# Layer-1 expert tiles loaded in pairs into ten slots, and the attention softmax taken by head from PSUM

## The reference

```
# layer 0
x += ssm(layernorm(x))                       # gated linear recurrence over time
x += xattn(layernorm(x), ctx, mask0)         # 16 heads of 16, 64 keys
x += layernorm(x) @ (W + V_r C).T + b
# layer 1
x += lstm_positions(layernorm(x))            # LSTM of 20 units, 512 steps; weights over earlier positions
x += xattn(layernorm(x), ctx, mask1) with weights * fside after the softmax
x += moe(layernorm(x))                       # 8 experts, top 1; leaky relu, squared; hidden 128

# the softmax of both attentions
scores = q @ k.T / 4
scores = where(mask0, scores, finfo.min)     # layer 0
scores = scores + (1 - mask1) * -1e9         # layer 1
attn = softmax(scores)                       # layer 1: then attn * fside
```

## Time and profile before

| | us |
|---|---|
| median of 3 runs (3178.17 to 3192.34) | 3188.12 |
| the profiled execution, its own time | 3191.33 |
| its span, first to last instruction | 3189.5 |

### The profile page before, as it was taken

How to read it: one execution, slowest core, us unless ns; L and a number is a source line. 1 busy time by engine, 2 the same in 40 slices (tenths; PEclk the granted TensorE clock), 3 DMA queues, 4 the chain that set the end, 5 groups by cost and what they waited for, 6 DMA issues and landing times.

```text
span 3189.5 us, 39732 instructions
## 1 busy us (share of the span) xinstructions
PE 2584.9 (81%) x11385; PEld 1542.6 (48%) x11385; DVE 1893.2 (59%) x6517; ACT 853.2 (27%) x2341; POOL 1317.4 (41%) x1372
## 2 busy tenths in 40 slices
PE   5799896977778778778778787999998868887945
PEld 3466453543636354635354545544544535544533
DVE  4576787768685767586768686645655414242311
ACT  0233242332232233223232332212222212122211
POOL 0363342324443345334444453423432545555534
PEclk9999896978786887678878786999899889899965
DMA  4110101020101110201010101111111253433032
GB/s 160 54 62 13 49 12 38 1 71 14 48 24 39 33 53 25 58 20 58 20 57 20 57 14 47 34 41 34 33 40 36 71 119 90 127 96 100 27 92 81
DMA packets 195337, 164.88 MB, mean 52 GB/s; under 512 B 52913, under 2 KB 188171, under 8 KB 194896
## 3 DMA queue, kind: packets, MB, share of 16 engines
q1 hardware_dynamic: 182352, 137.55, 14.6%
q0 software_dynamic: 12800, 25.27, 2.8%
HBM read 118.81 MB, written 51.80 MB: 53 GB/s over the span
## 4 chain that ended last, share of the span: by engine, by line
PE 36%; issue 21%; DVE 19%; POOL 12%; DMA 6%; SPq 3%; ACT 2%; POOLq 0%; DVEq 0%; ACTq 0%
PE p L775 4%; PE p L869 4%; PE p L832 4%; PE p L808 4%; PE p L769 3%; DVE l_xnat L1185 3%; PE p L786 3%; DMA out<-xy,xid 3%; DMA xw<-in_w_proj 3%; PE p L822 2%; POOL l_scratch L1547 2%; PE pg L841 2%; DVE ln_stats L1160 2%; PE p L849 2%; POOL l_scratch L1542 2%
## 5 line engine op out<-in xcount | busy, mean ns | idle before, releaser
L1521 POOL TENSOR_TENSOR ln_rstd<-ln_ve,neghalf 128x4 f32<-128x4 f32 x96 | 98.2, 1023 | 714.6 <-DVE ln_ve L1169 713.2
L1535 POOL TENSOR_TENSOR l_kbd<-l_kg,headmask 128x512 f32<-128x512 f32 x256 | 266.8, 1052 | 305.5 <-PE p L808 210.7
L1465 DVE SCALAR_TENSOR_TENSOR uin<-gates 16x20 f32<-16x20 f32 x512 | 175.5, 343 | 283.4 <-ACT gates L987 281.5
L832 PEld LDWEIGHTS p<-l_vg,l_scratch 128*128 128x128 f32 x2048 | 282.2, 215 | 75.0 <-issue 36.6
L987 ACT ACTIVATE gates<-pg 16x80 f32<-16x80 f32 x512 | 114.9, 224 | 761.0 <-PE pg L841 759.4
L1542 POOL TENSOR_TENSOR l_scratch<-l_scratch,l_mx 128x512 f32<-128x512 f32 x256 | 265.3, 1042 | 117.5 <-DVE l_mx L1215 116.7
L832 PE MATMUL p<-l_vg,l_scratch 128*128 128x34 f32 x2048 | 292.7, 296 | 15.9 <-ACT l_scratch L1016 6.8
L769 PE MATMUL p<-ident,l_xnat 128*128 128x128 f32 x1024 | 202.0, 339 | 123.2 <-DVE l_xnat L1185 122.0
L841 PE MATMUL pg<-wcat,slots 128*16 128x80 f32 x1024 | 177.2, 260 | 150.9 <-DVE slots L1477 149.0
L808 PE MATMUL p<-l_kbd,l_qT 128*128 128x512 f32 x512 | 275.6, 628 | 10.9 <-DVE l_scratch L1211 9.7
L841 PEld LDWEIGHTS pg<-wcat,slots 128*16 128x16 f32 x1024 | 59.0, 97 | 387.9 <-DVE slots L1477 238.5
(11 more groups left out here) (209 smaller groups left out, 4723.6 us busy)
## 6 DMA issues: line engine op xcount, KB each, us to landing
xln<-xln_dram SPq DMA_DIRECT2D x40, 512.0 KB, 4.4
l_vg<-v_dram SPq DMA_DIRECT2D x32, 544.0 KB, 4.0
x_dram<-l_xres SPq DMA_DIRECT2D x32, 512.0 KB, 3.6
xw<-in_w_fc SPq DMA_DIRECT2D x84, 128.0 KB, 2.2
xw<-in_w_proj SPq DMA_DIRECT2D x84, 128.0 KB, 2.5
l_kg<-k_dram SPq DMA_DIRECT2D x32, 256.0 KB, 4.3
xln_dram<-l_xnat SPq DMA_DIRECT2D x16, 512.0 KB, 3.0
l_xres<-x_dram SPq DMA_DIRECT2D x16, 512.0 KB, 5.5
```

The lines of the kernel that those rows point to most:

```text
L832: i = pe.matmul(o_bank[l][:, q * VW:(q + 1) * VW], w.exT[:, j, p, :], w.vg[:, b, q * VW:(q + 1) * VW], start=True, stop=True)
L1465: dve.scalar_tensor_tensor(uin[:, :], gates[:, 0:20], 1.0, gates[:, 60:80], ALU.add, ALU.mult)
L1535: pool.tensor_tensor(w.kbd[b % 2][:, j, :, :], w.kg[:, j, b:b + 1, :].broadcast_to([P, NE, SK]), headmask[:, :].rearrange("p (a o) -> p a ...
```

## The change

**Expert tiles.** Ten slots instead of four, and four output buffers instead of two. The slots take no new SBUF: weights go into the tiles of layer-0 weights (`wA` to `wO[0]`) and `tiles[0].xres`, rows into `tiles[0].xnat`, `xT`, `qT` and `kbd`, all free once lane 0 has ended. Two tiles are one step of SyncE; a pair shares the semaphores `m_in` and `m_rows`, so the first gather waits for the loads of both tiles and the first transpose for both gathers. The load of tile q waits for the expert matmul and scatter of tile q-10.

**Softmax.** `neg` becomes bf16 and its sign and that of q are turned, so that PSUM holds the negated scores. The mask is added on TensorE: a matmul of a bf16 identity (`same`) with `neg` broadcast over the 8 heads opens the accumulation, the score matmul closes it. VectorE takes the minimum from PSUM. ScalarE computes exp(-s + minimum) from PSUM with the minimum as per-partition bias, one instruction per head, 8 per unit, planned as four steps of two. "mask" and "shift" are gone. The next score into a bank waits for the eighth exp (`exped`), not for the mask. The sums stay on VectorE.

**Planner.** Costs are changed (see the diff), the hop after a DMA from 3 to 7 us, TILE_EVERY from 3.5 to 2.8 us. The spread is no longer given: `planned` tries 72 to 144 in steps of 8 and keeps the shortest plan. Stage 6 joins the stages with filler matmuls. Some semaphores are merged, and `orow` needs "keys" 7 instead of "shift" 7.

The core of the diff:

```diff
-TILE_SLOTS = 4
+TILE_SLOTS, OUT_SLOTS = 10, 4
...
-            ("pe", "score", u, 0.85, [("qland", u % 2), ("keys", u), ("mask", u - 2)]),
-            ("dve", "mask", u, 0.6, [("score", u), ("neg", 0), ("pturn", u - 4)] + ([("rows", 3)] if u == 0 and ahead else [])),
-            ("dve", "max", u, 0.6, [("mask", u)]),
-            ("pool", "shift", u, 1.0, [("max", u)]),
-            ("act", "exp", u, 0.5, [("shift", u)])]
+            ("pe", "score", u, 1.1, [("qland", u % 2), ("keys", u), ("neg", 0), ("exp", 4 * (u - 2) + 3)]),
+            ("dve", "max", u, 0.65, [("score", u), ("exp", 4 * (u - 4) + 3)] + ([("rows", 3)] if u == 0 and ahead else []))]
+        steps += [("act", "exp", 4 * u + e, 0.45, [("max", u), ("pturn", u - 4)])
+                  for e in range(4)]
...
+    for p in range(count // 2):
+        steps += [
+            ("clock", "due", p, 2 * every, [("due", p - 1)]),
+            ("sp", "mload", p, 5.6, [("due", p - 1), ("mexpert", 2 * p + 1 - TILE_SLOTS), ("mscatter", 2 * p + 1 - TILE_SLOTS)]),
+            ("dma", "mids", p, 0.1, [("mload", p)])]
+        steps += [("pool", "mgather", k, 1.3, [("mids", p), ("madd", k - TILE_SLOTS)]) for k in (2 * p, 2 * p + 1)]
+        steps += [("dma", "mrows", p, 0.1, [("mgather", 2 * p + 1)])]
...
-HOPS = {"pe": 0.22, "act": 0.2, "dve": 0.18, "pool": 0.1, "sp": 0.2, "dma": 3.0, "clock": 0.0}
-
-PACE = {0: (0.0, 4.0, 0.4), 1: (96.0, 16.0, 0.6), 2: (128.0, 4.0, 0.3), 3: (140.0, 0.0, 0.4), 4: (112.0, -18.0, 0.35),
-        5: (0.0, 22.0, 0.4), 6: (0.0, 0.0, 0.4)}
+HOPS = {"pe": 0.22, "act": 0.2, "dve": 0.18, "pool": 0.1, "sp": 0.2, "dma": 7.0, "clock": 0.0}
+
+PACE = {0: (4.0, 0.4), 1: (16.0, 0.6), 2: (4.0, 0.3), 3: (0.0, 0.4), 4: (-18.0, 0.35), 5: (22.0, 0.4), 6: (0.0, 0.4)}
...
-TILE_EVERY = 3.5
+TILE_EVERY = 2.8
...
-IDLE, FILL, WARM = 0.3, 0.9, (0, 4, 5)
+IDLE, FILL, WARM = 0.3, 0.9, (0, 4, 5, 6)
...
+    spreads = range(72, 152, 8) if 1 <= stage <= NC_ else (0,)
+    return min((planned_at(stage, ahead, spread) for spread in spreads), key=lambda plan: plan[0])[1]
...
-                        pe.wait_ge(t.masked, N - 1)
+                        pe.wait_ge(t.exped, N - 1)
+                    if u == 0:
+                        pe.wait_ge(t.neg, m + 1)
+                    pe.matmul(banks[l][j], same[:, :], w.neg[:, b:b + 1, :].broadcast_to([P, NE, SK]), start=True, stop=False)
                     pe.wait_ge(t.kbd, N + 1)
                     pe.matmul(banks[l][j], w.qT[:, j, b * P:(b + 1) * P],
-                              w.kbd[b % 2][:, j, :, :].rearrange("p a k -> p (a k)"), start=True, stop=True
+                              w.kbd[b % 2][:, j, :, :].rearrange("p a k -> p (a k)"), start=False, stop=True
                               ).then_inc(t.scores, 1)
...
-                    act.activation(ex, ex, ACT.Exp).then_inc(t.exped, 1)
...
+                    for h in (2 * e, 2 * e + 1):
+                        i = act.activation(w.ex[b % 2][:, NE * j + h, :], banks[lane][j][:, h * SK:(h + 1) * SK], ACT.Exp, scale=-1.0,
+                                           bias=w.mx[:, u % 4, h:h + 1])
+                    if e == 3:
+                        i.then_inc(t.exped, 1)
```

More of the change, by code:

```diff
@@ L38 @@
 EPS = 1e-5
[L39 removed]
+FMAX = 3.3895313892515355e38
 VW = 2 * HD + 2
@@ L120, in __init__ @@
         self.q, self.q_ready, self.kbd = sem(f"{name}_q"), sem(f"{name}_q_ready"), sem(f"{name}_kbd")
-        self.scores, self.masked, self.top = sem(f"{name}_scores"), sem(f"{name}_masked"), sem(f"{name}_top")
-        self.shifted, self.exped, self.summed = sem(f"{name}_shifted"), sem(f"{name}_exped"), sem(f"{name}_summed")
+        self.scores, self.top = sem(f"{name}_scores"), sem(f"{name}_top")
+        self.exped, self.summed = sem(f"{name}_exped"), sem(f"{name}_summed")
         self.gated, self.turned, self.exT = sem(f"{name}_gated"), sem(f"{name}_turned"), sem(f"{name}_exT")
@@ L189, in attention_steps @@
             ("dve", "o", u, 0.2 if l else 0.45, [("pv", u)] + ([("sums", u)] if l else []))]
-    steps += [("pool", "orow", 0, 2.3, [("shift", 7)])]
-    steps += [("pe", "oturn", h, 0.45, [("o", 4 * h + 3), ("mask", 7)]) for h in range(2)]
+    steps += [("pool", "orow", 0, 2.3, [("keys", 7)])]
+    steps += [("pe", "oturn", h, 0.45, [("o", 4 * h + 3), ("exp", 31)]) for h in range(2)]
     steps += [("act", "oland", h, 0.5, [("oturn", 1)]) for h in range(2)]
@@ L368, in planned @@
         kept.append((who, *key))
-    return kept
+    return max(end.values()), kept
 PLANS = {(stage, ahead): planned(stage, ahead) for stage in range(NC_ + 3) for ahead in (False, True)
@@ L443, in decoder_program @@
         tri = sb("tri", [P, P])
+        same = sb("same", [P, P], BF16)
         headmask = sb("headmask", [P, NE])
@@ L516, in decoder_program @@
         steps_row = sb("steps_row", [1, 2, 64])
-        xw = [sb(f"xw{i}", [P, 2 * D]) for i in range(TILE_SLOTS)]
-        xg = [sb(f"xg{i}", [P, 2 * D]) for i in range(TILE_SLOTS)]
+        whole = lambda w: w[:, :, :].rearrange("p h n -> p (h n)")
+        xw = [whole(w) for w in (wA, wB, wC, wD, wOut, wF, wQ[0], wO[0])]
+        parts = lambda w: [w[:, i:i + 2 * D] for i in range(0, 4 * D, 2 * D)]
+        done = tiles[0]
+        xw += parts(whole(done.xres))
+        xg = parts(whole(done.xnat)) + parts(whole(done.xT)) + parts(whole(done.qT))
+        xg += [t for w in done.kbd for t in parts(w[:, :, :, :].rearrange("p h a k -> p (h a k)"))]
         xid = [sb(f"xid{i}", [P, 2], I32) for i in range(TILE_SLOTS)]
@@ L523, in decoder_program @@
         xq = [sb(f"xq{i}", [P, P]) for i in range(2)]
-        xy = [sb(f"xy{i}", [P, D]) for i in range(2)]
+        xy = [sb(f"xy{i}", [P, D]) for i in range(OUT_SLOTS)]
         ctxA = xln[:, :, :, :].rearrange("p i b d -> p (i b d)").rearrange("p (h b k) -> p h b k", h=NH, b=B)
@@ L726, in _ @@
                             sp_step(lane, layer, family, index, c, g, n, m)
-            for i in range(2):
-                sp.wait_ge(o_store[i], 16 * (EARLY * TILES[0] + TILES[1]) // 2)
+            for i in range(OUT_SLOTS):
+                sp.wait_ge(o_store[i], 16 * (EARLY * TILES[0] + TILES[1]) // OUT_SLOTS)
         @block.tensor
@@ L793, in attention_step @@
                     if i_ == 0:
-                        pe.wait_ge(t.masked, 2 * GB * m + 2 * GB)
+                        pe.wait_ge(t.exped, 2 * GB * m + 2 * GB)
                     turn(l, i_, w.xnat, t.o_turned)
@@ L1240, in dve_step @@
                 s, l0, w = ln[lane], scans[lane], tiles[lane]
-                if family in ("neg", "mask", "max", "sums", "o", "add"):
+                if family in ("neg", "max", "sums", "o", "add"):
                     attention_step(lane, layer, family, i_, n, m)
```

139 lines of the change are left out of this document (64 added, 75 removed).

## The result

| | before | after |
|---|---|---|
| median, us | 3190.2 | 2934.7 |
| range of four runs, us | 3178.2 to 3193.2 | 2908.7 to 2951.0 |
| the profiled execution, its own time | 3191.3 | 2908.7 |
| its span | 3189.5 | 2906.9 |
| mean granted TensorE clock | 0.847 | 0.891 |

The ratio is 0.920, with a 95% interval of 0.912 to 0.928: 8% faster. (The median of before stands here with a fourth run.) The profiled execution of after is the quickest of its four, 26 us under their median, so sizes taken from the trace add up to 282.6 us, while the medians differ by 255.5.

What follows compares the result with a forecast made beforehand. Tiles were taken as bound by latency over slots, not work. Terms -39 (tail), -150 (tile bodies), +6, -6, -30, -55 and -2 sum to -276, giving 2912 us; range 2800 to 3035.

Steps and rivals of the forecast that it cites:

- (a): Whole kernel: tile laps shortened and stage 4 compressed, 2912 us, own range 2840 to 2970; chance 0.50.
- Tail: Last 24 expert tiles: ten slots remove the lap limit, 2.9 us a tile, -39 us (bounds -51 to -19).
- Three bodies: Stage 5's bodies with tiles: 115 us each plus 10 for the first's serial start, 355 against 505, -150 us.
- Stage 0, +6 and stage 1, -6: Stage 0 pays for added mask matmuls on TensorE; stage 1 gains from masks leaving VectorE, against more ScalarE work.
- Stages 2 and 3: Two-lane stages: queues, not the spread, set them; about 4 us a body kept from relieved engines, -30 us together.
- Stage 4: Stage sitting on its old spread of 112: the planner's search brings bodies from 119.5 to about 105 us, -55 us.
- The price of an exponential: ScalarE's softmax: a 64-column exp takes 0.31 us, 0.22 start to start, eight take 1.75 us.
- ScalarE's time hidden: All attention units: ScalarE gains 1.2 us a unit, 315 us in all, in no stretch its limit.
- (b): Only the tile part pays; queues hold stages 1 to 4: 3003 us, chance 0.20.
- (c): Re-planning pays everywhere, stages 1 to 5 and the tail: 2751 us, chance 0.17.
- (d): Tile lap not shortened: loads crowd each other, transfers lengthen, SyncE's pairs delay other loads; 3051 us, chance 0.08.
- (e): Slower: ScalarE bounds the two-lane stages, 3.0 us a unit, and LSTM tanh steps wait longer; 3352 us, chance 0.05.

Runs made afterwards that it cites:

- e1: The kernel before with the expert-tile part alone (ten slots, pairs, new tile costs, tail fillers), old softmax and spreads: 3043.0 us, ratio 0.956.
- e11: The whole change without filler matmuls in the tail: 2914.0 us, ratio 0.915 to the kernel before.
- e4: The whole change without the search for the LSTM's spread, old spreads kept: 3022.0 us, ratio 0.949 to the kernel before.
- e6: The whole change with VectorE's mask-sized sum put back ahead of each minimum, result unread: 2981.7 us, ratio 0.934 to the kernel before.
- e8: The whole change with one exponential of 512 columns per unit instead of eight, without the minimum as bias: 2829.6 us, ratio 0.890 to the kernel before.
- e9: As e8, but the minimum isn't taken at all and the exponential waits for the score: 2777.3 us, ratio 0.872 to the kernel before.
- e3: The kernel before with only the search for the LSTM's spread (72 to 144, shortest plan): 3180.0 us, ratio 0.999.
- e5: The kernel before with the search for the spread and the old softmax's steps planned at measured costs: 3176.1 us, ratio 0.996.
- e12: e8 with six unread exponentials of 64 columns put back on ScalarE behind each large one: 2848.6 us, ratio 0.893 to the kernel before.
- e10: The whole change with four slots in place of ten, still in pairs: 3157.3 us, ratio 0.991 to the kernel before.

## Why the prediction was right, and where its steps were not

2912 was forecast and 2935 measured, inside the range of 2800 to 3035 and of (a)'s own. That the sum lies so near is in part luck, since errors in it offset each other. By steps, against the profiled execution (282.6 us less):

- **Tail, -39 forecast, -33 in after's profile**, -40 in e1 and e11. The limit that comes next was named rightly: SyncE's 2.84 us a tile. The pace is 3.14 where 2.9 was forecast, and 2.77 in e11. First transpose 12.7 us behind the first load (11.8 forecast) and first sum 17.6 behind it (18.4 forecast).
- **Three bodies, -150 forecast, -131 in after's profile.** 115 a body held for the later two (119, 116). The mis-sized term is the serial start of the first: 138, 20 over the others, where 10 stood. The same bodies took 359 to 364 us in e4, e6, e8, e9 and e11, so part of the miss is this execution. GpSimd "over 75% busy" was wrong: it is at 70 to 72% in the two good bodies and 60% in the first.
- **Stage 0, +6 and stage 1, -6:** +6 and -2.
- **Stages 2 and 3, -30 forecast, -50 by the profile.** The sum was right in sign and too small, and its reason failed: without the search it is +2 (e4), and with it and the old softmax +23 (e3). I had written that queues and not the spread set these stages, and booked the 30 for the softmax alone. It takes both, the softmax and the search.
- **Stage 4, -55 forecast, -69.** 102 us a body where 105 stood. Here the size was right and the owner wrong. I gave it to the search alone; alone it takes 35, and the whole kernel gains nothing that can be told (e3). The stage needs true costs (e5, -59) or the new softmax besides (after).
- **The last body, -2:** -4.
- **The price of an exponential.** 0.31 us long, 0.22 apart and 1.85 from the first start to the last end were forecast; 309 ns and 1.75 were measured, (1.75 - 0.31) / 7 = 0.21 apart. The Trainium skill ("ScalarE: Activation LUTs", section "What ACT_TABLE_LOAD costs"), by which it would be 0.33 and 0.24 apart, is a little high for these, which read PSUM. The trace agrees that the fixed part is the price: 64 columns take 309 ns, and 512 without a bias 0.60 us in e8.
- **ScalarE's time hidden: the step that failed.** I let 315 us of short pieces cost nothing because ScalarE is in no stretch the limit. Its busy share indeed stays at or under 46% in every stretch, and still the pieces cost 105 us (e8), some 19 of them, 32 at most, as occupancy (e12). What I had worked out and then not used was the other sentence, on the bank held for 4.2 us and the chain of 2.5. The exponentials' 1.15 us more in the chain should have stood in the sum as a cost of the two-lane stages 2 and 3: 64 units on each lane there, one behind the other, would make 74 us (an estimate), and 81 were measured. Over all units it would be too much, since stages 0, 1 and 4 show no loss. The forecast stood all the same because errors offset. In stages 2 to 4 I had booked 55 us for the search and 30 for the softmax. The softmax without the search brought nothing there (+11, e4), the search on top of it 130, and the small exponentials cost 73 of what could have been gained (after against e8).
- **Engine totals.** ScalarE 1170 forecast, 1108 measured; VectorE 1720 and 1765; GpSimd 1050 and 1063.
- **The rivals.** (b), 3003, fell: stages 2 to 4 gave 119 us. (c), 2751, is where e9 comes near, with work left out that after has. (d) fell with the wait at 57.9 us; where the lap does stay, in e10, the wait is 331.1 us and the time 3157, beyond (d)'s 3051. (e) had the right suspect in the right place and the wrong limit: a unit of exponentials takes 1.75 us and not 2.5, and the LSTM's stage 1 is 2 us shorter than before.

## What to carry to other kernels

When tiles wait for a slot, divide the lap by the number of slots, and then look for the queue that becomes the next limit; here it was the issuing of the loads, and it could be read from two loads that followed each other freely. An operation split into small ones costs by its place: in the chain between score and weights it can cost as latency even on an engine that is busy 40% of the time, here in the two stages where both lanes and the LSTM stand side by side and not in the others, and the test is to put the same work back behind the chain. Parts that bring nothing alone can bring much together, and what a better plan gains in one stage has to be checked against the whole time, and against the granted clock, before it is counted.

## What the runs showed of the hardware that I had not expected

TensorE's busy time for the same 4280 matmuls was 994.5 us in after and 942.4 in e8, at mean granted clocks of 0.84 and 0.87: a few gaps fewer (30 us) came with more than their own length in quicker matmuls. In e12 18 of the 30 us of gaps were back, with 953.0 us busy at 0.87, so the gaps' total does not tell the clock. In the tail the clock went from 0.67 to 0.92 with fillers and the time did not move, since the loads there wait for no slot and follow each other at 3.17 us (after) and 2.96 us (e11). And an exponential of 64 columns with bias took 309 ns and 0.21 us from start to start from PSUM (after, above), but 336 ns and (1.05 - 0.34) / 3 = 0.24 us from SBUF in e12, so PSUM was not the dearer source. The first line is from the groups of e12, the second from its timeline:

```profile
L1038 ACT ACTIVATE junk<-ident,ones 128x64 f32<-128x64 f32 x1536 | 409.9, 336 | 0.0
...
1409.11 1.05 ACT L1038 ACTIVATE junk<-ident,ones 128x64 f32<-128x64 f32 x4
```
